# The start of attention shared by two engines, and softmax sums normalised in SBUF instead of through DRAM

## The reference

```python
q, k, v = (split_heads(h @ W + b) for W, b in ((Wq, bq), (Wk, bk), (Wv, bv)))      # h = layernorm(x)
scores = einsum('bhqd,bhkd->bhqk', q, k) / scale
c2p = take_along_axis(einsum('bhqd,hpd->bhqp', q, pos_k), clip(rel + 64, 0, 127))
p2c = take_along_axis(einsum('bhkd,hpd->bhkp', k, pos_k), clip(-rel + 64, 0, 127)).swapaxes(-1, -2)
probs = softmax(scores + (c2p + p2c) / scale)
out = layernorm((probs @ v).merge_heads() @ Wo + bo + h) * ln_scale + ln_bias
x = x + layernorm(out)
x = x + layernorm(experts(layernorm(x)))        # argmax of a softmax over 8, relu(x @ W1 + b1) @ W2 + b2
```

## Time and profile before

| | us |
|---|---|
| median of 3 runs | 1844.06 (1834.3 to 1849.8) |
| profiled execution | 1851.49 |
| its span | 1849.6 |
| TensorE busy | 1664.1 (90%) |
| VectorE busy | 1432.0 (77%) |
| ScalarE busy | 1163.0 (63%) |
| GpSimd busy | 1062.1 (57%) |
| DMA | 426.33 MB, mean 230 GB/s |

### The profile page before, as it was taken

How to read it: one execution, slowest core, us unless ns; L and a number is a source line. 1 busy time by engine, 2 the same in 40 slices (tenths; PEclk the granted TensorE clock), 3 DMA queues, 4 the chain that set the end, 5 groups by cost and what they waited for, 6 DMA issues and landing times. The chain is left out here.

```text
span 1849.6 us, 41173 instructions
## 1 busy us (share of the span) xinstructions
PE 1664.1 (90%) x13688; PEld 1132.0 (61%) x13688; DVE 1432.0 (77%) x4124; ACT 1163.0 (63%) x2784; POOL 1062.1 (57%) x1264
## 2 busy tenths in 40 slices
PE   7954799999989999989999998999977875999997
PEld 4532565666656666656666665666633554999996
DVE  4752798999979999979999997999945854555553
ACT  6844577888868887867887876887752641222221
POOL 0002777777767777876777776787713622333332
PEclk9985899999989999999999998999995867999998
DMA  4977788888868888886878887778618724666661
GB/s 143 314 256 232 256 273 267 265 266 270 270 223 273 272 266 261 267 264 231 280 253 274 261 258 234 251 273 279 200 38 211 236 90 147 200 196 205 194 202 64
DMA packets 297948, 426.33 MB, mean 230 GB/s; under 512 B 35766, under 2 KB 239308, under 8 KB 297643
## 3 DMA queue, kind: packets, MB, share of 16 engines
q1 hardware_dynamic: 286504, 393.28, 65.9%
q10 hardware_dynamic: 7491, 21.10, 3.6%
q0 software_dynamic: 3744, 9.31, 1.4%
HBM read 245.85 MB, written 178.05 MB: 229 GB/s over the span
## 5 line engine op out<-in xcount | busy, mean ns | idle before, releaser
L874 ACT ACTIVATE t_probsT<-t_flip 128x512 f32<-128x512 f32 x1024 | 626.0, 614 | 232.9 <-PE t_flip L762 141.8
L812 DVE TENSOR_REDUCE t_most<-t_scores 128x1 f32<-128x640 f32 (+1 forms) x512 | 434.4, 848 | 80.2 <-PE t_scores L739 77.7
L831 DVE TENSOR_SCALAR t_band<-t_band,t_top 128x384 f32<-128x384 f32 (+1 forms) x512 | 420.6, 822 | 0.0
L776 PE MATMUL t_sum_ps<-t_probsT,t_vals 128*32 128x256 f32 x4096 | 329.2, 393 | 0.2 <-ACT t_probsT L874 0.2
L866 ACT COPY t_table<-t_table_ps 128x388 f32<-128x388 f32 x512 | 248.0, 484 | 49.9 <-PE t_table_ps L713 49.9
L950 POOL TENSOR_TENSOR t_near<-t_near,masks 128x768 f32<-128x768 f32 (+1 forms) x128 | 272.9, 2132 | 0.0
L934 POOL TENSOR_TENSOR t_near<-t_near,masks 128x384 f32<-128x384 f32 (+1 forms) x128 | 147.7, 1154 | 215.1 <-DMA t_near<-skew_d 212.0
L732 PE MATMUL t_scores<-t_afters,t_quests 105*128 105x256 bf16 (+3 forms) x1024 | 245.5, 289 | 24.9 <-DVE t_most L816 24.9
L762 PE MATMUL t_flip<-masks,t_band 128*128 128x128 f32 x1408 | 261.5, 275 | 0.0
L816 DVE CUSTOM_DVE_ANT_0 t_band<-t_scores,t_near 128x384 f32<-128x384 f32 (+1 forms) x512 | 261.1, 510 | 0.0
L739 PE MATMUL t_scores<-masks,t_near 128*128 128x128 f32 x1408 | 244.3, 277 | 5.8 <-POOLq L953 5.8
(11 more groups left out here) (206 smaller groups left out, 2597.9 us busy)
## 6 DMA issues: line engine op xcount, KB each, us to landing
skew_d<-t_table SPq DMA_DIRECT2D x128, 1024.0 KB, 11.5
t_near<-skew_d SPq DMA_DIRECT2D x128, 640.0 KB, 8.2
t_near<-skew_d SPq DMA_DIRECT2D x128, 384.0 KB, 7.5
e_w<-in_L_ffn_W_dram ACTq DMA_DIRECT2D x39, 512.0 KB, 4.0
e_w<-in_L_ffn_W_dram SPq DMA_DIRECT2D x39, 512.0 KB, 3.8
split_d<-p_part SPq DMA_DIRECT2D x32, 384.0 KB, 3.3
t_afters<-split_d SPq DMA_DIRECT2D x128, 96.0 KB
t_quests<-split_d SPq DMA_DIRECT2D x128, 96.0 KB
```

What stands on the lines that cost most here:

```text
L776: last = nc.tensor.matmul(sum_ps[32 * g:32 * g + 32, 0:2 * P], vals[b % 2][:, j, h * VDIM:h * VDIM + 32], probsT[s % 3][:, g * 2 * P:(g + ...
L812: nc.vector.tensor_reduce(most[:, c, 1:2], out[:, wide:S], AX.X, ALU.max)
L831: nc.vector.tensor_scalar(band[n % 2][:, t, 0:wide], band[n % 2][:, t, 0:wide], top[n % 2][:, t:t + 1], None, ALU.subtract).then_inc(level ...
L874: nc.scalar.activation(probsT[s % 3][:, half * 512:(half + 1) * 512], flip_ps[half][:, :], ACT.Exp, scale=SCALE).then_inc(expd, 1)
```

## The change

1. Of the first twenty tables the even ones go through `table_ps` and ScalarE as before; the odd ones are made in the second score bank, `scores_ps[1]`, and copied by VectorE with two `tensor_copy`. Table x waits for table x - 2. `score(1)` waits until VectorE has copied its ten.
2. The hats' and values' buffers belong to a new class `Hats` that is allocated around `project` and `attend`. SP loads units 0 to 3, far rows 0 and 2 and the first values in `project`, between its last stores (s = 5, 6, 7). The loop in `attend` starts at u = -2.
3. `look` and `level` are interleaved otherwise: reduce of s, level of s - 1, TTR of s, whose start value is the reduce's result, so that its accumulator is the top. The tiny maximum goes. Level becomes `tensor_scalar` with an accumulator output that nobody reads.
4. The sums are normalised in SBUF: `normalise(n)` is a shuffle that spreads the sum's row over the head's rows (128 x 256), a reciprocal (128 x 256) and a `tensor_tensor` multiplication (128 x 256) on VectorE, behind the look of s = 8n + 23 (a tile 7), and for the last two units behind the last level. `store` waits for it, and comes one unit later. `load_totals`, `invert` and `store_share` go, and `share_d`.
5. `mix` loads no shares and no totals; `share_heads` goes, and `project_out` reads `heads` as they land.

```diff
+class Hats:
...
+            hats = Hats(nc, held, ctx)
             project(nc, sem, x, Wq, bq, Wk, bk, Wv, bv, rel_emb, c_pick, c_masks, c_side, pick_d, split_d, far_d, v_d,
-                    masks, inv_all, rows)
+                    masks, inv_all, rows, hats)
...
+                if s == 5:
+                    for i in range(2):
+                        sp.wait_ge(v_out[i], 16)
+                        sp.wait_ge(split_out[i], 16 * 8)
+                        sp.wait_ge(far_out[i], 16)
+                    hats.load_unit(sp, split_d, 0)
+                    hats.load_unit(sp, split_d, 1)
+                if s == 6:
+                    hats.load_far(sp, far_d, 0)
+                    hats.load_vals(sp, v_d, 0)
+                    hats.load_unit(sp, split_d, 2)
+                if s == 7:
+                    hats.load_unit(sp, split_d, 3)
+                    hats.load_far(sp, far_d, 2)
...
-                if 0 <= u - 2 < N:
-                    store(u - 2)
-                if u % BATCH == 2 and 1 <= u // BATCH < B:
-                    load_totals(u // BATCH - 1)
-                if u % BATCH == 4 and 1 <= u // BATCH < B:
-                    store_share(u // BATCH - 1)
-                if u == -1:
-                    load_vals(0)
+                if 0 <= u - 3 < N:
+                    store(u - 3)
...
-                if x >= 1:
-                    pe.wait_ge(table_kept, x)
+                if x > AHEAD:
+                    pe.wait_ge(table_kept, by_act(x - 1))
+                elif x >= 2 and x % 2 == 0:
+                    pe.wait_ge(table_kept, by_act(x - 2))
+                elif x >= 2:
+                    pe.wait_ge(early_kept, by_dve(x - 2))
+                out = table_out(x)
...
+                if s == 1:
+                    pe.wait_ge(early_kept, AHEAD // 2)
...
-                nc.vector.tensor_reduce(most[:, c, 1:2], out[:, wide:S], AX.X, ALU.max)
+                if s >= 2:
+                    dve.wait_ge(seen, s - 1)
+                nc.vector.tensor_reduce(most[:, c:c + 1], out[:, wide:S], AX.X, ALU.max).then_inc(far_seen, 1)
+                if s >= 1:
+                    level(s - 1)
...
-                nc.vector.tensor_tensor_reduce(band[n % 2][:, t, 0:wide], out[:, 0:wide],
-                                               near[n % 2][:, 0, t, at:at + wide], 1.0, -3.0e38, ALU.add, ALU.max,
-                                               accum_out=most[:, c, 0:1]).then_inc(seen, 1)
-                dve.wait_ge(seen, s + 1)
...
-                nc.vector.tensor_scalar(peak[:, c, :], most[:, c, :], 1.0, None, ALU.mult, ALU.max,
-                                        accum_out=top[n % 2][:, t:t + 1]).then_inc(peaked, 1)
+                dve.wait_ge(far_seen, s + 1)
+                nc.vector.tensor_tensor_reduce(band[n % 2][:, t, 0:wide], out[:, 0:wide],
+                                               near[n % 2][:, 0, t, at:at + wide], 1.0, most[:, c:c + 1], ALU.add, ALU.max,
+                                               accum_out=top[n % 2][:, t:t + 1]).then_inc(seen, 1)
...
                 nc.vector.tensor_scalar(band[n % 2][:, t, 0:wide], band[n % 2][:, t, 0:wide], top[n % 2][:, t:t + 1],
-                                        None, ALU.subtract).then_inc(leveled, 1)
+                                        None, ALU.subtract, ALU.max, accum_out=junk[:, s % 2:s % 2 + 1]
+                                        ).then_inc(leveled, 1)
+
+            def normalise(n):
+                dve.wait_ge(sum_kept, n + 1)
+                if n >= 1:
+                    dve.wait_ge(normed, n)
+                nc.vector.stream_shuffle(spread[:, :], made[n % 2][:, :], [DH] * 32).then_inc(spread_made, 1)
+                dve.wait_ge(spread_made, n + 1)
+                nc.vector.reciprocal(spread[:, :], spread[:, :]).then_inc(inverse_made, 1)
+                dve.wait_ge(inverse_made, n + 1)
+                nc.vector.tensor_tensor(made[n % 2][:, :], made[n % 2][:, :], spread[:, :], ALU.mult).then_inc(normed, 1)
...
-            def invert(b):
-                dve.wait_ge(totals_in, 16 * (b + 1))
-                if b >= 1:
-                    dve.wait_ge(share_out, 16 * b)
-                nc.vector.reciprocal(inverse[:, :], totals[:, :]).then_inc(inverse_made, 1)
-
+            BEHIND = QT + LAG + 2
+            for x in range(1, AHEAD, 2):
+                dve.wait_ge(table_made, x + 1)
...
+                nc.vector.tensor_copy(ends, out[:, :, 0:FEW].rearrange("p a (e v) -> p a e v", e=2))
+                nc.vector.tensor_copy(wide[:, :, LEFT:SPOT - LEFT],
+                                      out[:, :, LEFT - 1:LEFT].to_broadcast([P, 2, SPOT - FEW])).then_inc(early_kept, 1)
             for s in range(TS):
-                if s % (QT * BATCH) == 3 * QT and s >= QT * BATCH:
-                    invert(s // (QT * BATCH) - 1)
                 look(s)
-                if s >= 1:
-                    level(s - 1)
+                if s >= BEHIND and (s - BEHIND) % QT == 0:
+                    normalise((s - BEHIND) // QT)
             level(TS - 1)
+            for n in range((TS - 1 - BEHIND) // QT + 1, N):
+                normalise(n)
...
-                pool.wait_ge(peaked, QT * (n + 1))
+                pool.wait_ge(seen, QT * (n + 1))
...
-            def share_heads(g):
-                dve.wait_ge(heads_in[g % BUFS], 64 * (g // BUFS + 1))
-                if g >= 2:
-                    dve.wait_ge(out_made, g - 1)
-                nc.vector.tensor_tensor(headsT[g % 2][:, :, :], heads[g % BUFS][:, :, :], share[g % BUFS][:, :, :], ALU.mult
-                                        ).then_inc(headsT_made, 1)
-
...
             def project_out(g):
-                pe.wait_ge(headsT_made, g + 1)
+                pe.wait_ge(heads_in[g % BUFS], 32 * (g // BUFS + 1))
```

More of the change, by code:

```diff
@@ L43 @@
 XROWS = KROWS + 9
+ROW = DH * PARTS
+FAR = KROWS + PARTS
+MROW = XROWS
+ROWS = XROWS + PARTS
+BUFS = 6
+HATS = 4
+FARS = 2
+EARLY = 4
 EPS, EPS_ATT = 1e-5, 1e-7
@@ L174, in project @@
 def project(nc, sem, x, Wq, bq, Wk, bk, Wv, bv, rel_emb, c_pick, c_masks, c_side, pick_d, split_d, far_d, v_d,
-            masks, inv_all, rows):
+            masks, inv_all, rows, hats):
     G = 512
@@ L571, in attend @@
         made = [sb(f"made{i}", [P, 2 * P]) for i in range(2)]
-        totals, inverse = sb("totals", [P, P]), sb("inverse", [P, P])
+        spread, junk = sb("spread", [P, 2 * P]), sb("junk", [P, 2])
         scores_ps = [ps(f"scores{i}", [P, S]) for i in range(2)]
@@ L597, in live, with by_act, by_dve, wait_tables @@
             return 0 <= s < TS
+        def by_act(x):
+            return x // 2 + 1 if x < AHEAD else x - AHEAD // 2 + 1
+        def by_dve(x):
+            return (min(x, AHEAD - 1) + 1) // 2
+        def wait_tables(engine, x):
+            engine.wait_ge(table_kept, by_act(x))
+            if x < AHEAD + 2 * QT:
+                engine.wait_ge(early_kept, by_dve(x))
+        def table_out(x):
+            return scores_ps[1][:, 0:512].rearrange("p (a v) -> p a v", a=2) if x < AHEAD and x % 2 else table_ps
+        def parts_of(x):
+            n, u = x // QT, x % QT
+            wide = table[n % 2][:, u // 4, :, u % 4, :]
+            return view(wide.tensor, wide.offset, [list(wide.ap[0]), list(wide.ap[1]), [SPOT - LEFT, 2], [1, LEFT]]), wide
         def band_of(t):
@@ L863, in keep_table @@
                     act.wait_ge(side_kept, (n - 2) * 2 + h + 1)
-                wide = table[n % 2][:, h, :, u % 4, :]
-                ends = view(wide.tensor, wide.offset, [list(wide.ap[0]), list(wide.ap[1]), [SPOT - LEFT, 2], [1, LEFT]])
+                ends, wide = parts_of(x)
                 nc.scalar.copy(ends, table_ps[:, :, 0:FEW].rearrange("p a (e v) -> p a e v", e=2))
@@ L904, in _ @@
                     exponent(back, 0)
-                if live(s + AHEAD):
+                if live(s + AHEAD) and (s >= 0 or s % 2 == 0):
                     keep_table(s + AHEAD)
@@ L918, in keep_side @@
             def keep_side(n, h):
[L919 removed]
+                wait_tables(pool, n * QT + 4 * h + 3)
                 if n >= 3:
@@ L1170, in _ @@
             dve.wait_ge(ready, 4)
-            dve.wait_ge(totals_in, 16)
-            nc.vector.reciprocal(inverse[:, :], totals[:, :]).then_inc(inverse_made, 1)
             dve.wait_ge(bo_in, 16)
@@ L1187, in _ @@
                                            ALU.mult, ALU.add).then_inc(bo_made, 1)
-            for g in range(2):
-                share_heads(g)
             residual(0)
```

139 lines of the change are left out of this document (61 added, 78 removed).

## The result

Over 20 runs each the changed kernel has a median of 1839.1 us (1834.4 to 1843.8), the kernel before 1844.7 (1834.3 to 1858.6): 5.6 us less, where 26 were forecast. The ratio is 0.9961, with a 95% interval of 0.9944 to 0.9977. The profiled executions are further apart than the medians: 1851.49 before, 1839.39 after, spans 1849.6 and 1837.5.

A forecast was written before the change was run, and what follows sets the result against it. The prediction took TensorE to bound the attention loop, VectorE 3% behind. Its terms, -9 - 8 + 0.5 - 32 + 37 + 2.6 - 2 - 15 = -26 us, brought the median from 1844.06 to 1818, range 1782 to 1852.

The forecast's parts named there:

- Bound and pace: Attention loop: TensorE is the bound with VectorE 3% behind; turned tops at a steady interval of 18.4 us.
- the burst: Normalisation on VectorE behind the look at tile 7: 0.6 us per unit, over 61 units +37 us (bounds 12 and 73).
- The stalls: Attention loop: three waits at the reciprocal of the totals, with the half clock behind them, all go: -32 us.
- the second rival: Attention loop: near tables' chain through SP sets the pace, 18.4 us per unit; 1818 to 1830 us, chance 0.12.
- The start: Start to first near matmul: earlier tables less the cost of SP's added DMAs in projection, together -8.5 us.
- +0.5: Projection: some 20 more DMA issues by SP, spread over three gaps of its cycle, cost +0.5 us (0 to 2).
- The gain of 9 us: Start of attention: earlier first copy and two engines copying tables in turn save 9 us (7 to 15).
- Mix: Mix stage: without share_heads residual steps go from 6.0 to 5.0 us, -15 us (bounds -5 and -22).
- the likeliest case: Whole kernel: the forecast itself, median 1818 us, own range 1800 to 1836, chance 0.43.
- The case of "same": Whole kernel: time within about 1%, 18 us, of the kernel before, between 1826 and 1862; chance 0.22.
- the four rivals: Loop: burst nearly hidden (1786, chance 0.26), near chain paces (0.12), burst dearer (1854, 0.13), level no faster (1875, 0.06).

The follow-up runs named there:

- experiment 2: The changed kernel with the normalisation (shuffle, reciprocal, multiplication) left out and products stored as they are; 1806.0 us, ratio 0.9795 to the kernel before.
- experiment 6: The kernel before with the reciprocal of a batch's totals 16 looks later and the store of its inverses two rounds later; 1829.7 us, ratio 0.9878.
- experiment 12: The kernel before with the later reciprocal of the totals and the change's new look and level, sums still through DRAM; 1828.2 us, ratio 0.9896.
- experiment 10: The changed kernel with the multiplication on GpSimd and only unit 0's hats loaded in projection, the others in attention; 1802.4 us, ratio 0.9760.
- Experiments 1: The changed kernel with all hats loaded at the start of attention, as in the kernel before; 1835.8 us, ratio 0.9969 to the kernel before.
- experiments 9: The changed kernel with the multiplication on GpSimd and all hats loaded in attention; 1804.7 us, ratio 0.9785 to the kernel before.
- experiment 5: The changed kernel with the normalisation's multiplication moved from VectorE to GpSimd; 1804.0 us, ratio 0.9757; second run on another chip 1802.2 us, ratio 0.9762.

## Why the prediction was wrong, and where it was right

**Bound and pace: right.** TensorE was the bound with VectorE behind it, and the burst between two looks was named as what would cost. It was forecast at 18.4 per unit, and came at 18.54. Of the forecast's 6.4 us of VectorE against 5.96 and a wait of 0.3, the wait of the multiplication was 0.45 and came in every unit, not in half of them: GpSimd's mask follows the splits, these follow the look at tile 7, and so does the multiplication. The two are locked, so a mean over random phases was the wrong way to work out the wait. Single prices: shuffle 0.44 (forecast 0.36), reciprocal 1.75 (1.8), multiplication 0.42 undisturbed (0.40), level 0.60 (0.56), and the TTR, whose start value is now a column of SBUF, 0.61 where the earlier trace rows had 0.55.

**The stalls: right in the sum, and not for the stalls alone.** With the burst left out the intervals of the changed kernel take 32.4 us less than in the first profile before (experiment 2: 1127.3 against 1159.7), where 33.5 were forecast. But the stalls are not all of it: in the kernel before, their removal alone gives 18 to 23 us in the loop (experiment 6), and intervals above 17.82 appear elsewhere, together with more waiting for near tables and splits, which speaks for the second rival at a third of its size. The other 10 us come with other parts of the change, and with which is open (experiment 12).

**The start: wrong, the step that failed.** The prediction booked +0.5 us for "some 20 DMAs more" of SP "spread over three gaps of its cycle". It counted the issues at the price of an issue in an empty queue. Each group of eight stores behind them took 7.5 to 9.3 us instead of 4.45, the following group came later, and again found loads ahead of it; the last store was 12.7 us later. Projection ended later still: the first table of attention is at 153.98, where experiment 10, whose last stores are as before, has it at 135.54. So this term was 18.4 us, not 0.5.

The gain of 9 us was there behind it. In the changed kernel and in experiment 10 the first copy follows the first table by 7.2 us, behind ScalarE's own DMA issues, as the forecast had it; without the queue it would come at 142.74 (forecast 142.45) instead of 146.03. From the first copy to the first near matmul are 26.8 us before (146.03 to 172.83) and 18.9 in the changed kernel (161.18 to 180.07). These 7.9 and the 3.3 of the first copy are 11.2, and 18.4 less 11.2 is the measured +7.2. (The first profile before flatters the 3.3: in the second one the first copy is at 143.31.)

Experiments 1 and 10 don't show this gain, because they are rid of the queue by moving hats back into attention: their first near matmul is only 2 us (169.4) and 4 us (167.2) earlier than before (171.4, the mean of the two profiles). There SP issues hats between the two writes of the first unit's tables. In experiment 10 the eight tables are copied by 147.8 (forecast 147.5), but the second write goes out at 151.04:

```profile
142.74 0.49 ACT L913 COPY t_table<-t_table_ps 128x388 f32<-128x388 f32 x1 [17.49 <-issue]
```
```profile
145.15 0.55 SPq L678 DMA_DIRECT2D skew_d<-t_table  x1
145.74 2.00 SPq L178 DMA_DIRECT2D afters<-split_d  x2
147.78 1.88 SPq L178 DMA_DIRECT2D quests<-split_d  x2
...
151.04 0.55 SPq L678 DMA_DIRECT2D skew_d<-t_table  x1
```

In the changed kernel it follows the first by 2.7 us (163.58 and 166.30). The next stretch says the same: from the first near matmul to the first turned top are 20.5 us with the hats loaded in projection, and 26.9, 27.0 and 26.7 in experiments 1, 9 and 10, against 26.5 before. So the hats cost about as much in the one place as in the other. At the first turned top the changed kernel is 1.2 us behind the first profile before, experiments 1 and 10 are 3.0 and 5.5 ahead of it, where 15 were forecast; in the medians of experiments 9, 10 and 5 (its second run) nothing of this difference is left that can be told. No run has the hats early and the stores undisturbed.

**Mix: right in size, by half for another reason.** -15 was forecast from TensorE's floor, -15.4 measured, but by the profiles at equal clock only about 8 of it is the shorter chain, and the rest came with the clock of that execution.

**From profile to median.** The forecast took the difference of two profiled executions for that of the medians. The first lay 7 us above its median, the second at it. -12 in the profiles is -6 in the medians. A second profile of the kernel before also lay 6 above; the traces show stalls of different length and mix at different clocks, and in the two profiles of experiment 5 three quarters of their difference are in mix. But no execution of the kernel before near its median has a profile, so what makes it faster isn't shown.

**The range** of 1782 to 1852 holds the result, the likeliest case's own, 1800 to 1836, does not. The case of "same", which came, had 0.22; none of the four rivals is what happened, since none of them doubted the start's +0.5.

## What to carry to other kernels

Work that is moved into a gap of a queue is to be priced by what stands behind it in the queue, not by its own issue: four transfers fitted, seven or eight made the next eight take up to twice as long. A short operation that hangs on the same event as another engine's longer one, and waits for its end, waits every time and not by chance (0.45 us in each unit here); moved to the engine that it waited for, it cost nothing that shows. And a stall at a late transfer is first to be tried with a later consumer: two changed numbers gave 1.2%, where the rebuilt path gave 0.4% until its multiplication was moved (2.4%). The old place has its price too: the same loads, left in attention, stood ahead of a write that the first scores waited for. The two prices have to be set against each other.

## What the runs showed that was not expected

- A tensor_scalar of 384 columns with an accumulator output takes 0.60 us and in the loop never more than 0.606; the plain one takes 0.42 alone and 0.79 in the mean beside GpSimd. Where VectorE sets the pace, the kernel with the slower form is 119 us faster.
- A multiplication on VectorE with both inputs in SBUF ended 0.28 us after GpSimd's mask in all 61 cases in which it began within it, and took 0.42 in the three without one.
- Once VectorE sets the pace, 53 of 63 intervals between units lie within 0.05 us (18.52 to 18.56); between the stalls of the kernel before they went from 17.8 to 20.5.
- The same stage at the same work took 91 and 98 us in two profiles of one kernel, at granted clocks of 0.73 and 0.63.
